# Step pictures of 46 of 98 histogram groups from differences on TensorE, and group one-hots in 16-bit pairs

## What is computed

```python
t1 = x @ W1
msg = (t1[src] + (x[src] * x[dst]) @ W2) / (sqrt(out_deg[src]) * sqrt(out_deg[dst]))[:, None]
agg = segment_sum(msg, dst)
embed = leaky_relu(where(in_cnt > 0, t1 + agg, 0) + b, 0.01)
embed = embed / max(norm(embed), 1e-12)
out = layernorm(x + embed)
```

## Time and profile before

| | us |
|---|---|
| median of 3 runs (1108.18 to 1111.76) | 1109.14 |
| the profiled execution, its own time | 1105.97 |
| its span, first to last instruction | 1104.1 |
| mean granted TensorE clock | 0.915 |

### The profile page before, as it was taken

One profiled execution on the slowest core, in us unless ns is written; L12 is line 12 of the kernel. 1 busy time (PEld: TensorE's weight loads), 2 busy tenths in 40 slices (PEclk: granted clock), 3 DMA queues, 4 the chain that ended last, 5 costly groups with the idle time before them and its releaser, 6 DMA issues.

```text
span 1104.1 us, 31256 instructions
## 1 busy us (share of the span) xinstructions
PE 927.1 (84%) x13011; PEld 819.3 (74%) x13011; DVE 722.0 (65%) x1523; ACT 480.1 (43%) x1357; POOL 684.5 (62%) x651
## 2 busy tenths in 40 slices
PE   3376650299899999999999999999999999999893
PEld 2265540278788888888888888888888888888782
DVE  8999999835366555566566566656556567467443
ACT  5899967423233333333334333334333333333311
POOL 4400000377777777777777777777777777777720
PEclk9985555589999999999999999999999999999997
DMA  9100004655555545555555555555555555555520
GB/s 313 59 2 1 2 2 177 229 148 146 158 154 165 161 142 165 153 161 164 164 147 163 165 159 162 164 166 155 164 160 154 167 159 158 159 157 167 152 82 21
DMA packets 68120, 155.83 MB, mean 141 GB/s; under 512 B 12006, under 2 KB 37668, under 8 KB 67972
## 3 DMA queue, kind: packets, MB, share of 16 engines
q0 software_dynamic: 40144, 123.12, 39.4%
q1 hardware_dynamic: 27828, 30.65, 8.5%
HBM read 137.69 MB, written 16.03 MB: 139 GB/s over the span
## 4 chain that ended last, share of the span: by engine, by line
POOL 52%; issue 18%; DVE 13%; PE 13%; DMA 2%; ACT 0%; POOLq 0%; DVEq 0%; ACTq 0%
POOL y_rows L681 52%; PE g_ps L814 6%; DVE hi_hot L329 4%; DVE lo_hot L338 3%; PE emb_ps L852 2%; DVE xs L420 2%; PE grp_ps L776 2%; DMA y_rows<-y_parts,idx_tab 1%; DVE yp L406 1%; PE win_ps L795 1%; DMA yp<-in_spans_dram,widx 1%; DVE yp L305 1%; PE hist_ps L510 1%; DMA y_parts<-yp 0%; DVE yp L412 0%
## 5 line engine op out<-in xcount | busy, mean ns | idle before, releaser
L681 POOL DMA_INDIRECT y_rows<-y_parts,idx_tab x616 | 660.5, 1072 | 192.6 <-issue 185.5
L814 PE MATMUL g_ps<-yp,counts 128*128 128x256 bf16 (+1 forms) x4410 | 571.4, 274 | 0.0
L814 PEld LDWEIGHTS g_ps<-yp,counts 128*128 128x128 f16 x4410 | 408.6, 98 | 49.4
L710 ACT CAST counts<-win_ps 128x392 f16<-128x392 f32 x480 | 230.4, 484 | 465.0 <-PE win_ps L795 463.6
L923 DVE TENSOR_TENSOR key_hot<-iota_h,pairs 128x1568 f16<-128x1568 f16 x120 | 116.9, 974 | 279.8 <-PE win_ps L795 278.4
L795 PE MATMUL win_ps<-key_hot,lo_hot 128*128 128x98 f16 x1920 | 168.7, 211 | 50.8 <-DVE lo_hot L923 49.8
L795 PEld LDWEIGHTS win_ps<-key_hot,lo_hot 128*128 128x128 f16 x1920 | 131.3, 100 | 71.5 <-DVE lo_hot L923 50.8
L923 DVE TENSOR_TENSOR lo_hot<-iota_h,pairs 128x2048 f16<-128x2048 f16 x120 | 146.8, 1223 | 37.2 <-PE win_ps L795 36.3
L776 PEld LDWEIGHTS grp_ps<-hot,y_rows 128*128 128x128 bf16 x3696 | 104.0, 97 | 39.6 <-DMA y_rows<-y_parts,idx_tab 37.4
L776 PE MATMUL grp_ps<-hot,y_rows 128*128 128x48 bf16 x3696 | 108.0, 184 | 30.2 <-DMA y_rows<-y_parts,idx_tab 30.0
L445 ACT ACTIVATE yp<-iota_b,half_lo 128x128 bf16<-128x128 bf16 x416 | 122.3, 402 | 0.8 <-PE step_ps L510 0.8
(11 more groups left out here) (123 smaller groups left out, 668.4 us busy)
## 6 DMA issues: line engine op xcount, KB each, us to landing
y_rows<-y_parts,idx_tab POOLq DMA_INDIRECT x616
y_parts<-yp SPq DMA_DIRECT2D x6, 1344.0 KB, 5.1
xs<-in_x_dram SPq DMA_DIRECT2D x1, 6144.0 KB
xb<-in_x_dram SPq DMA_DIRECT2D x48, 128.0 KB
out_dram<-o_sb SPq DMA_DIRECT2D x48, 128.0 KB
src_i<-in_src_t_dram SPq DMA_DIRECT2D x1, 784.0 KB, 5.1
y_parts<-yp SPq DMA_DIRECT2D x1, 768.0 KB, 4.3
y_parts<-yp SPq DMA_DIRECT2D x1, 576.0 KB, 5.5
```

Of the source, the lines that this page charges most:

```text
L681: nc.gpsimd.indirect_dma_start(out=y_rows[:, g % RING, t, :], out_offset=None, in_=y_dram[:, :], in_offset=bass.IndirectOffsetOnAxis(ap=id ...
L710: nc.scalar.copy(counts[:, c % 2, :, i * WN:(i + 1) * WN], win_ps[:, i % 2, 0:KEYS].rearrange("p (d s) -> p s d", s=BLOCKS)).then_inc(s_cn ...
L814: last = nc.tensor.matmul(g_ps[:, c % 2, 0:n], counts[:, c % 2, s, :], yp_1[:, s, m * D:m * D + n], start=(s == 0 and m == PARTS - 1), sto ...
```

## The change

1. The signed groups are now 46 of 98: 1, 3, 5, 7, 9, 11, 13 of every 15.
2. The step pictures of a signed group come from differences. PE multiplies a 17-row piece of `rows_lo` (the lo parts of 16 tiles as rows, and a row of ones) with `select` (-1 where the row is the tile's own, n + 0.5 in the last row) in four matmuls of 512 columns, which gives n + 0.5 - lo for 16 tiles in two halves of diff_ps. ACT takes the sign of a half in one ACTIVATE of 128x1024 from PSUM. Two halves replace the 16 ACTIVATEs of 128x128 and half_lo.
3. PE issues the differences of a signed group g before the histograms of g - 3 and g - 2 (`diff_at`), and waits before each for ACT's same half of the signed group before.
4. Two tables are new inputs: rows_t (128x1536 int32) and select (128x2048 bf16), loaded on SP's queue before dst. DVE masks rows_t (128x1536) between the two parts of the bits; ACT casts it to rows_lo.
5. PSUM is parted anew: base_ps and below_ps share one bank (PE waits for widx before it writes the base), wt_ps has one buffer for two, and the batches of transposes come every third group.
6. rel is kept twice side by side, so that `hot` (128x384) is one comparison of 16-bit pairs with iota_h; iota_f goes.

```diff
@@ -49,18 +49,19 @@
 HT = 16
 HI_COLS = 50
 HI_RING = 4
-SIGN_PERIOD = 11
-SIGN_GROUPS = (3, 7, 10)
+SIGN_PERIOD = 15
+SIGN_GROUPS = (1, 3, 5, 7, 9, 11, 13)
+STEP_ROWS = 32
-TURN_STEP = 2
+TURN_STEP = 3
...
         ident = sb("ident", [P, P], F32)
         ones_b = sb("ones_b", [P, 1], BF16)
-        iota_f = sb("iota_f", [P, W], F32)
-        rel = sb("rel", [P, GT], F16)
+        rel = sb("rel", [P, GT, 2], F16)
...
-        s_differ = sem("s_differ"); s_bits = sem("s_bits"); s_pairs1 = sem("s_pairs1"); s_half = sem("s_half")
+        s_differ = sem("s_differ"); s_bits = sem("s_bits"); s_pairs1 = sem("s_pairs1"); s_rows_t = sem("s_rows_t"); s_sel = sem("s_sel")
+        s_rowbits = sem("s_rowbits"); s_rowlo = sem("s_rowlo"); s_diff = sem("s_diff")
...
-            half_lo = sb1("half_lo", [P, TT], F32)
+
+            rows_lo = sb1("rows_lo", [P, ROW_SETS, P], BF16)
+            sel = sb1("sel", [P, HT * P], BF16)
...
+            rows_i = words[:, 2 * WWORDS:2 * WWORDS + ROW_SETS * P]
...
-            base_ps = ps1("base_ps", [P, 512])
+            small_ps = ps1("small_ps", [P, 512])
+            base_ps, below_ps = small_ps[:, 0:2 * P], small_ps[:, 2 * P:4 * P]
             hist_ps = ps1("hist_ps", [P, 512])
-            below_ps = ps1("below_ps", [P, 512])
             step_ps = ps1("step_ps", [P, 512])
-            wt_ps = ps1("wt_ps", [P, 2, 512])
+            wt_ps = ps1("wt_ps", [P, 512])
+            diff_ps = ps1("diff_ps", [P, 2, HT * P // 4 * 2])
...
+            HALF = HT * P // 2
+            diff_at = {}
+            for i, g in enumerate(signed):
+                for half in range(2):
+                    diff_at.setdefault(max(0, g - 3 + half), []).append((i, half))
...
+                    sp.dma_start(rows_i[:, :], rows_t[:, :]).then_inc(s_rows_t, 16)
+                    sp.dma_start(sel[:, :], select[:, :].bitcast(BF16)).then_inc(s_sel, 16)
                     sp.dma_start(dst_f[:, :], dst_t[:, 0:GT]).then_inc(s_dst, 16)
...
-                    for t0, t1 in PAIR_PARTS:
+                    for part, (t0, t1) in enumerate(PAIR_PARTS):
                         nc.vector.tensor_single_scalar(bits[:, 0, t0:t1], src_i[:, t0:t1], P - 1, ALU.bitwise_and)
                         nc.vector.tensor_single_scalar(bits[:, 1, t0:t1], src_i[:, t0:t1], 7,
                                                        ALU.arith_shift_right).then_inc(s_bits, 1)
+                        if part == 0:
+                            dve.wait_ge(s_rows_t, 16)
+                            nc.vector.tensor_single_scalar(rows_i[:, :], rows_i[:, :], P - 1, ALU.bitwise_and
+                                                           ).then_inc(s_rowbits, 1)
                     nc.vector.tensor_copy(iota_b[:, :], iota_i[:, :])
-                    nc.vector.tensor_copy(iota_f[:, :], iota_i[:, 0:W])
...
-                        nc.vector.tensor_tensor(rel[:, :].rearrange("p (g t) -> p g t", t=TILES),
-                                                dst_f[:, :].rearrange("p (g t) -> p g t", t=TILES),
-                                                base_ps[:, 0:GT // TILES].unsqueeze(2)
-                                                .to_broadcast([P, GT // TILES, TILES]), ALU.subtract)
+
+                        for k in range(2):
+                            nc.vector.tensor_tensor(rel[:, :, k].rearrange("p (g t) -> p g t", t=TILES),
+                                                    dst_f[:, :].rearrange("p (g t) -> p g t", t=TILES),
+                                                    base_ps[:, 0:GT // TILES].unsqueeze(2)
+                                                    .to_broadcast([P, GT // TILES, TILES]), ALU.subtract)
...
-                        dve.wait_ge(s_half, 1)
+                        dve.wait_ge(s_pairs1, 2 * len(PAIR_PARTS))
+                        dve.wait_ge(s_rowlo, 1)
...
-                    nc.scalar.activation(half_lo[:, :], bits[:, 0, :], ACT.Copy, scale=-1.0, bias=0.5
-                                         ).then_inc(s_half, 1)
-                    act.wait_ge(s_half, 1)
-                    act.wait_ge(s_setup, 4)
+                        if i == 0:
+                            act.wait_ge(s_rowbits, 1)
+                            nc.scalar.copy(rows_lo[:, :, :].rearrange("p c e -> p (c e)"), rows_i[:, :]
+                                           ).then_inc(s_rowlo, 1)
 
                     def steps(i):
                         if i >= 2:
                             act.wait_ge(s_hist, signed[i - 2] + 1)
-                        for t in range(HT):
-                            last = nc.scalar.activation(lo_step[:, i % 2, t, :], iota_b[:, :], ACT.Sign,
-                                                        bias=half_lo[:, signed[i] * HT + t:signed[i] * HT + t + 1])
-                        last.then_inc(s_step, 1)
+                        for half in range(2):
+                            act.wait_ge(s_diff, 2 * i + half + 1)
+                            nc.scalar.activation(lo_step[:, i % 2, half * HT // 2:(half + 1) * HT // 2, :]
+                                                 .rearrange("p t n -> p (t n)"), diff_ps[:, half, :], ACT.Sign
+                                                 ).then_inc(s_step, 1)
...
-                        nc.scalar.copy(tab[:, k, s * P:(s + m) * P], wt_ps[:, b % 2, 0:m * P]).then_inc(s_wtc, 1)
+                        nc.scalar.copy(tab[:, k, s * P:(s + m) * P], wt_ps[:, 0:m * P]).then_inc(s_wtc, 1)
...
+                    pe.wait_ge(s_widx, 1)
                     pe.wait_ge(s_dst, 16)
...
-                            pe.wait_ge(s_step, i + 1)
+                            pe.wait_ge(s_step, 2 * i + 2)
...
-                        if b >= 2:
-                            pe.wait_ge(s_wtc, b - 1)
+                        if b >= 1:
+                            pe.wait_ge(s_wtc, b)
                         for i in range(m):
-                            last = nc.tensor.transpose(wt_ps[:, b % 2, i * P:(i + 1) * P],
+                            last = nc.tensor.transpose(wt_ps[:, i * P:(i + 1) * P],
                                                        wkey[:, k, s + i, :], ident[:, :])
                         last.then_inc(s_wtr, 1)
 
+                    def differences(i, half):
+
+
+                        if i == 0 and half == 0:
+                            pe.wait_ge(s_rowlo, 1)
+                            pe.wait_ge(s_sel, 16)
+                        if i >= 1:
+                            pe.wait_ge(s_step, 2 * i + half - 1)
+                        q = i % (P // STEP_ROWS) * STEP_ROWS
+                        for m in range(2):
+                            at = half * HALF + m * 512
+                            last = nc.tensor.matmul(diff_ps[:, half, m * 512:(m + 1) * 512],
+                                                    rows_lo[q:q + HT + 1, i // (P // STEP_ROWS), :],
+                                                    sel[q:q + HT + 1, at:at + 512], start=True, stop=True)
+                        last.then_inc(s_diff, 1)
+
                     for g in range(HIST_GROUPS):
+                        for i, half in diff_at.get(g, ()):
+                            differences(i, half)
                         if g in turn_at:
                             turn_lists(turn_at[g])
                         histogram(g)
...
-                        nc.vector.tensor_tensor(hot[:, g % 2, :, :],
-                                                iota_f[:, 0:W].unsqueeze(1).to_broadcast([P, TILES, W]),
-                                                rel[:, g * TILES:(g + 1) * TILES].unsqueeze(2)
-                                                .to_broadcast([P, TILES, W]), ALU.is_equal).then_inc(s_hot, 1)
+                        nc.vector.tensor_tensor(
+                            hot[:, g % 2, :, :].rearrange("p t (c two) -> p t c two", two=2),
+                            iota_h[:, 0:W].rearrange("p (c two) -> p c two", two=2).unsqueeze(1)
+                            .to_broadcast([P, TILES, W // 2, 2]),
+                            rel[:, g * TILES:(g + 1) * TILES, :].unsqueeze(2).to_broadcast([P, TILES, W // 2, 2]),
+                            ALU.is_equal).then_inc(s_hot, 1)
...
+    signed = [g for g in range(tiles // HT) if g % SIGN_PERIOD in SIGN_GROUPS]
+    per = P // STEP_ROWS
+    rows_t = _np.ones((-(-len(signed) // per), per, STEP_ROWS, P), _np.int32)
+    for i, g in enumerate(signed):
+        rows_t[i // per, i % per, :HT] = padded['src'].reshape(tiles, P)[g * HT:(g + 1) * HT]
+    select = _np.zeros((STEP_ROWS, HT, P), _np.float32)
+    select[_np.arange(HT), _np.arange(HT)] = -1.0
+    select[HT] = _np.arange(P) + 0.5
+    select = (select.view(_np.uint32) >> 16).astype(_np.uint16).reshape(STEP_ROWS, HT * P)
     for name, a in (('src_t', padded['src'].reshape(tiles, P).T),
                     ('dst_t', padded['dst'].reshape(tiles, P).T.astype(_np.float32)),
-                    ('starts', starts), ('spans', spans)):
```

(16 more changed lines are left out.)

## The result

The changed kernel is slower: 1141.86 us against 1108.66 (medians of 4 runs each), ratio 1.0305 with a 95% interval of 1.025 to 1.0361. The profiled execution took 1146.91 us with a span of 1145.1, 41.0 more than the span before.

What follows compares the result with a forecast made beforehand. DVE was taken to bound stage 1, POOL's gathers stage 2. Against the profiled 1105.97 us, -19.3 + 0.5 + 1 + 2 + 0.3 - 3.0 = -18.5; from the median 1109.14 this gave 1091, likeliest 1084 to 1098, 8 in 10 1081 to 1110.

Steps and rivals of the forecast that it cites:

- The step that failed: PE in stage 1: with differences busy 12.5 of 16.4 us, 76%, it was taken to hold the fast clock.
- slow for more than half of the stage: Rival, PE in groups 16 to 97: at the slow clock over half the stage, slower; always slow 1128; chance 0.11.
- My 39 signed groups: PE after list_keys: 39 signed groups at 1.72 us each in the always-slow sum of 128.2 us.
- a rival of its own: PE: each change between weights of 128 and 17 rows empties it, 0.7 us a signed group; 1096; chance 0.08.
- The rule on the clock: PE in stage 1: fast clock is given up after a spell of idleness; by this it would hold.
- DVE's part: Groups from 16 on: DVE's comparisons take 88.6 us instead of 107.9, 19.3 less, if DVE stays the bound.
- My losses of 1 and 2 us behind list_keys: After list_keys: 1 us while PE is slow, 2 us for groups 17 to 40, nearly level with DVE.
- the 3.0 us for hot: Stage 2 gathers: hot at 0.36 us instead of 0.55 delays fewer gathers; 3.0 us gained (0 to 5).
- ACT was right: ACT in stage 1: sign of 1024 columns takes 1.0 us, 14.0 per 15 groups against DVE's 16.4, so hidden.
- Before group 16: Start of stage 1: nothing won; list_keys at 41.6, 0.5 us late, bounds 40.5 and 44.

Runs made afterwards that it cites:

- the burst: Changed kernel plus 14 matmuls of 128 rows x 512 columns in PE's pause before group 16, then the 17-row differences as before: 1139.37 us.
- The run of hot alone: Kernel before with only the comparison for hot in 16-bit pairs and rel kept twice: 1110.65 us against 1109.19, ratio 1.0016.
- both halves together: Changed kernel with both halves of a signed group's differences issued together, before the histogram three groups ahead: 1133.56 us, ratio to before 1.0186.
- the run in which ACT clears select: Changed kernel with 128 rows in each difference, ACT instead of POOL clearing select at the start: 1089.45 us, ratio 0.9822.

## Why the prediction was wrong, by its steps

- **The step that failed** is "a slow PE here never rests, and work without rest was granted the clock each time", with "I take it that it holds". Every grant in the trace of before came after work of matmuls with all 128 rows. I priced the 17-row matmuls by their columns alone, asked only whether PE would be busy, and gave "slow for more than half of the stage" 0.11. PE was busy without a break for 139 us (55.5 to 194.9) and was never granted the fast clock. The same program with 128 rows has it within 5 us, with 64 after 17.5, with 32 not at all.
- **The rival that came true was priced too low**, 1128. Its 128.2 us left out the cost of a change between 17 and 128 rows, which I had as a rival of its own at 0.7 us a signed group and 0.08. It is four times 0.11, 0.43 us: two groups take 3.49, of which two histograms are 1.34 and four matmuls 1.72. My 39 signed groups were too many too: differences go out two to three groups ahead, so those of group 16 and half of those of group 18 lie before the stage, and 37.5 are left. 82 x 0.66 + 37.5 x (1.72 + 0.43) + 7 = 142 us, and PE's stretch as measured is 141.5 (55.55 to 197.1). The two rivals were not alternatives: both held at once. The row I used against it, narrow weights at 225.00, says nothing of short ones, and that the trace has no change in rows was wrong: 38 matmuls of one row stand in stage 2, such as these.

```profile
325.80 0.38 PE L829 MATMUL g_ps<-ident,gb 128*128 128x128 f32 x2
326.11 0.38 PE L830 MATMUL g_ps<-ones_f,cb 1*128 1x1 f32 x2
```

  The two of 128 rows start 0.11 us apart (0.38 for both, 0.27 for one), the first of one row 0.20 after the second of them. The shapes are others, but the extra 0.09 was there to be read, and points to this rival. The Trainium skill's rule on changes of the tiling mode (page "TensorEngine Tiling (Array Packing)", section "Key Properties") agrees with these rows: 0.11 us at each change with 17 rows, about the same with 32 and 64, none seen with 128.
- **The rule on the clock.** That the fast clock is given up after a spell of idleness (the Trainium skill, page "TensorE: Matmul & The Clock Gate", section "The HAM clock gate") agrees with two rows: with 128 rows the clock was lost in a pause of 2.77 us, with the burst right behind one of 2.96. But it leaves the changed kernel unexplained, which was busy throughout and not granted, and the kernel before: raised at 63.6, it was lost at 70.4 though no wait in between was longer than 0.87 us:

```profile
70.19 0.71 PE L510 MATMUL hist_ps<-hi_hot,lo_hot 128*128 128x50 bf16 x16 [0.87 <-DVE lo_hot L338]
```

  Where the rule and these rows differ, the rows decide.
- **DVE's part was right.** 88.6 us for the groups from 16 on were forecast; 88.9 and 89.0 were measured where PE did not bind. My losses of 1 and 2 us behind list_keys did not come there. The forecast of 1091 is close to what the kernel takes once its differences use all rows (1089), but part of that is luck: the 3.0 us for hot and the 3 us of losses, both absent, cancel in the sum.
- **ACT was right**: 1.0 us forecast, 1.02 measured, and its waits are PE's.
- **Before group 16**: list_keys at 41.6, bound 44; it came at 43.5, since slow PE held DVE from 35 us on (waits of 0.47 and 1.59 us), and with fast PE at 42.1, on the spans as argued.
- **hot**: the size of the operation and of its own delays was right, the gain of 3.0 was wrong. It assumed that a gather freed from one delay keeps the time. The run of hot alone shows no gain, and in its trace the lateness moved to the long comparisons.

## What to carry to other kernels

Price a new matmul by its rows as well as by its columns. A few rows don't make it cheaper, they can keep the fast clock from all matmuls around it, and each change to and from full rows costs time; padding with zeros to all 128 rows made the same work 53 us shorter here. Before a forecast leans on the clock, look which matmuls stood before each grant in the trace, and read the level from the durations: the clock column says nothing ahead of its first change. Where two rivals can hold at once, add them.

## What the runs showed of the hardware that was not expected

- The clock went with the rows driven, though the products of the added rows were zeros: with 17 and 32 rows it was never granted among the differences of the profiled executions (but for the burst), with 64 after 17.5 us, with 128 after 4.4 us.
- It is not wholly fixed: the runs with the burst and with both halves together each had one launch of four that was shorter, by 22 and 13 us than its run's median, and of which there is no profile.
- One launch of the run in which ACT clears select (46 signed groups) took 1903 us; its four others took 1084 to 1090. Its profile has PE at the slow clock from first to last, in stage 2 too, where it is dense with full matmuls:

```profile
L865 PE MATMUL g_ps<-yp,counts 128*128 128x256 bf16 (+1 forms) x4410 | 1126.1, 447 | 0.0
```

It is 571.4 us and 274 ns in the kernel before. Why the clock never rose in that launch was not found.
- Clearing 128x4096 f32 on POOL for 3.5 us held up a DVE cast of 128x98 for as long, as the gathers are held up by DVE's comparisons in the other direction. Who began first may decide: POOL began at 3.20 and the cast at 3.25. In the run with 64 rows the cast began at 3.22, POOL's clearing of 128x2048 at 3.30, and the cast took 0.21 us as ever.
